# Filling the key stacks by way of HBM, and spreading a chunk's maxima evenly, in a two-layer perceiver kernel

## The reference

```python
x = x + _L0_xattn_ref(_layernorm(x), ctx_768, ...)   # q from x; k, v from the context; softmax over 12544
x = x + _L0_attn_ref(_layernorm(x), ...)             # Mamba
x = x + _L0_ffn_ref(_layernorm(x), ...)
x = x + _L1_xattn_ref(_layernorm(x), ctx_768, ...)   # the same shape of work again
x = x + _L1_attn_ref(_layernorm(x), ...)             # linear attention
x = x + _L1_ffn_ref(_layernorm(x), ...)
```

## Time and profile before

| | |
|---|---|
| median of three runs | 1404.1 us |
| the profiled execution's own time | 1412.64 us |
| its span | 1410.9 us |
| TensorE (PE) busy | 1151.9 us, 82% |
| VectorE (DVE) busy | 738.6 us, 52% |
| ScalarE (ACT) busy | 711.6 us, 50% |
| GpSimd (POOL) busy | 415.1 us, 29% |
| DMA moved | 147.04 MB, 104 GB/s over the span |

### The profile page before, as it was taken

One profiled execution on the slowest core, in us unless ns is written; L12 is line 12 of the kernel. 1 busy time (PEld: TensorE's weight loads), 2 busy tenths in 40 slices (PEclk: granted clock), 3 DMA queues, 4 the chain that ended last, 5 costly groups with the idle time before them and its releaser, 6 DMA issues.

```text
span 1410.9 us, 30285 instructions
## 1 busy us (share of the span) xinstructions
PE 1151.9 (82%) x13033; PEld 815.1 (58%) x13033; DVE 738.6 (52%) x1358; ACT 711.6 (50%) x991; POOL 415.1 (29%) x256
## 2 busy tenths in 40 slices
PE   6769899999999988315897769999999998989556
PEld 6446566666666645215696346666666666656345
DVE  4536565555565562678225536555555555563431
ACT  3336566666666546251212246666666666657210
POOL 3444444444444200042003444444443343300000
PEclk8689999999999999658898679999999999999668
DMA  7977777878787660610804977777777787760803
GB/s 147 140 104 98 99 101 104 108 100 111 104 111 98 72 148 2 210 60 3 295 1 96 135 109 97 100 104 103 101 105 101 99 110 100 86 120 2 297 24 64
DMA packets 88134, 147.04 MB, mean 104 GB/s; under 512 B 10040, under 2 KB 77568, under 8 KB 87488
## 3 DMA queue, kind: packets, MB, share of 16 engines
q1 hardware_dynamic: 87104, 144.98, 64.0%
q10 hardware_dynamic: 896, 0.12, 0.1%
HBM read 66.74 MB, written 0.18 MB: 47 GB/s over the span
## 4 chain that ended last, share of the span: by engine, by line
PE 65%; DVE 18%; issue 6%; DMA 5%; ACT 3%; POOL 2%; SPq 0%; ACTq 0%; DVEq 0%; POOLq 0%
PE ring L605 32%; PE st L605 16%; PE ot L605 15%; DVE mpart L1277 8%; DMA qst<-rowb 4%; DVE arena L1404 2%; PE ring L740 1%; ACT arena L983 1%; DMA arena<-scratch_perm 1%; DVE arena L1408 1%; DVE arena L1263 1%; DVE nmb L1285 1%; DMA wkv<-L_wkv 0%; SPq L398 0%; PE ring L611 0%
## 5 line engine op out<-in xcount | busy, mean ns | idle before, releaser
L1277 DVE TENSOR_REDUCE mpart<-ring 128x1 f32<-128x448 f32 x896 | 516.7, 619 | 435.2 <-PE ring L605 433.0
L1006 ACT ACTIVATE work<-st 128x1024 f32<-128x1024 f32 x392 | 401.6, 1024 | 242.9 <-PE st L605 236.7
L605 PE MATMUL ring<-arena,qst 96*128 96x448 bf16 x896 | 305.5, 375 | 12.5 <-issue 6.3
L605 PE MATMUL ot<-work,arena 128*17 128x128 f32 x6272 | 262.6, 284 | 29.2 <-issue 27.5
L605 PE MATMUL st<-qst,arena 97*128 97x128 bf16 x3136 | 249.6, 223 | 33.2 <-DMA qst<-rowb 18.1
L605 PEld LDWEIGHTS st<-qst,arena 97*128 97x128 bf16 x3136 | 202.2, 100 | 98.9 <-issue 42.7
L523 POOL TENSOR_TENSOR arena<-arena 128x896 f32<-128x896 f32 x52 | 98.2, 1888 | 519.4 <-ACT arena L979 519.4
L605 PEld LDWEIGHTS ot<-work,arena 128*17 128x17 f32 x6272 | 142.4, 99 | 131.6 <-issue 92.4
L605 PE MATMUL ring<-ctxr,wkvr 128*128 128x448 f32 x560 | 171.9, 451 | 38.5 <-POOL ctxr L554 24.2
L605 PE MATMUL ring<-wkvr,ctxr 128*128 128x256 f32 x980 | 150.4, 299 | 8.6 <-ACT arena L990 4.2
L605 PEld LDWEIGHTS ring<-ctxr,wkvr 128*128 128x128 f32 x560 | 124.8, 229 | 54.7 <-issue 34.2
(11 more groups left out here) (281 smaller groups left out, 787.2 us busy)
## 6 DMA issues: line engine op xcount, KB each, us to landing
arena<-arena SPq DMA_DIRECT2D x336, 224.0 KB, 11.2
arena<-ffn_W SPq DMA_DIRECT2D x16, 1024.0 KB, 12.1
warena<-ctxT SPq DMA_DIRECT2D x28, 448.0 KB, 14.2
warena<-ctxT SPq DMA_DIRECT2D x56, 224.0 KB, 14.9
arena<-f SPq DMA_DIRECT2D x2, 4096.0 KB, 25.0
arena<-scratch_bc SPq DMA_DIRECT2D x1, 2048.0 KB, 7.3
arena<-scratch_perm SPq DMA_DIRECT2D x2, 1024.0 KB, 9.7
arena<-rows SPq DMA_DIRECT2D x1, 1792.0 KB, 7.0
```

The costliest lines, as they stand in the source:

```text
L605: return nc.tensor.matmul(o, l, r, start=start, stop=stop, **kw)
L1006: nc.scalar.activation(pbuf[:, n % 2], st[:, 2 * (n % 2):2 * (n % 2) + 2].rearrange("p b k -> p (b k)"), ACT.Exp).then_inc(*signal(f"{lay} ...
L1277: V.reduce_max(mpart[:, 2 * h + hf:2 * h + hf + 1], ring[:, BANKS[step][0], 0:HALF], AX_X).then_inc(*signal(f"{lay}_b_max"))
```

## The change

The stack of a chunk is filled in two moves instead of one. First the three parts and two halves of `kparts` are written to a new tensor in HBM, `scratch_k` (two buffers), by six transfers of 128 rows of 1792 bytes. When all six have landed (`parts_out`), twelve transfers fill the stack from there, each one slot and one half of the heads: 16 rows of 14336 bytes, since in HBM the values of 8 heads lie one behind the other. The wait for the stack's old scores stands between the writes and the loads; before the writes stands a wait for the loads that last read this buffer of `scratch_k`. A half is now heads 0 to 7 or 8 to 15, so the maxima go in the plain order of heads and `head_of` is gone. ScalarE's `k1` waits for `parts_out` of the chunk before, once per chunk. And `per_unit` becomes (2, 3, 2, 3, 2, 2, 3, 2, 3) and (2, 2, 2, 2, 2): of a chunk's 32 maxima 10 instead of 17 are taken in units 9 to 13.

```diff
+PARTS = 16 * 3 * KC
...
-        per_unit = ((4,) * 8 + (0,) if c == 0 else (1, 1, 1, 1, 3, 2, 2, 2, 2)) + (3, 4, 3, 4, 3)
+        per_unit = ((4,) * 8 + (0,) if c == 0 else (2, 3, 2, 3, 2, 2, 3, 2, 3)) + (2, 2, 2, 2, 2)
...
-def head_of(n):
-
-    return n // 2 % (H // KC) * KC + n // H, n % 2
...
+        scratch_k = nc.dram_tensor("scratch_k", [2, 3, P, KC, CK], BF16).ap()
...
             def stack(lay, c):
 
                 b = c % KBUFS
+                if c >= 2:
+                    for half in range(2):
+                        sp.wait_ge(sem(f"{lay}_kst{half}_in"), STACK * (c - 1))
+                for part in range(3):
+                    for m in range(KC):
+                        sp.wait_ge(*of(lay, f"k{part + 1}_done", KC * c + m + 1))
+                        load(scratch_k[c % 2, part, :, m], kparts[:, part, m * CK:(m + 1) * CK], f"{lay}_parts_out")
                 if c >= KBUFS:
                     sp.wait_ge(sem(f"{lay}_s_full"), (c - KBUFS + 1) * UNITS)
-                for m in range(KC):
-                    for part in range(3):
-                        sp.wait_ge(*of(lay, f"k{part + 1}_done", KC * c + m + 1))
-                        for s in range(SLOTS):
-                            if K_SPLIT[s] == part:
-                                load(kst[HD * s:HD * (s + 1), b].rearrange("l (h m) k -> l h m k", m=KC)[:, :, m],
-                                     kparts[:, part, m * CK:(m + 1) * CK], f"{lay}_kst{m}_in")
+                sp.wait_ge(sem(f"{lay}_parts_out"), PARTS * (c + 1))
+                for half in range(2):
+                    heads = slice(half * H // 2, (half + 1) * H // 2)
+                    groups = slice(half * H // 2 // KC, (half + 1) * H // 2 // KC)
+                    for s in range(SLOTS):
+                        load(kst[HD * s:HD * (s + 1), b, heads].rearrange("l h k -> l (h k)"),
+                             scratch_k[c % 2, K_SPLIT[s]].rearrange("(l g) m k -> l g (m k)", l=HD)[:, groups]
+                             .rearrange("l g n -> l (g n)"), f"{lay}_kst{half}_in")
...
                     if kind == "b":
-                        h, hf = head_of(n)
+                        h, hf = n // 2, n % 2
...
                     if kind == "k1":
                         act.wait_ge(sem(f"{lay}_k_out"), 4 * c + 2 * n + 2)
-                        if c:
-                            act.wait_ge(sem(f"{lay}_kst{n}_in"), STACK * c)
+                        if n == 0 and c:
+                            act.wait_ge(sem(f"{lay}_parts_out"), PARTS * c)
...
-                        h, hf = head_of(n)
-                        V.reduce_max(mpart[:, 2 * h + hf:2 * h + hf + 1], ring[:, BANKS[step][0], 0:HALF], AX_X
+                        V.reduce_max(mpart[:, n:n + 1], ring[:, BANKS[step][0], 0:HALF], AX_X
```

## The result

The changed kernel took 1484.4 us (median of four runs, 1474.0 to 1493.8), the kernel before 1404.7 beside it. The ratio is 1.056, with a 95% interval of 1.047 to 1.065: slower by 5.6%, some 80 us. The forecast was 1493 us, 89 slower. The profiled execution has a span of 1479.6 us against 1410.9. The traces are of single executions; that of after_row_first (experiment 4) is 18 us slower than its median, and no wait is read from it.

A forecast was written before the change was run, and what follows sets the result against it. PE's work was taken to set most of the time, the rest short holes. Terms +29 +72 -19 -11 +18 = +89 took the profiled 1412.6 to 1501.7, which lies 8.5 above the median, giving 1493 us; range 1350 to 1590.

The forecast's parts named there:

- The rate of the loads: Stack loads from HBM: stay at 123 GB/s despite longer rows, because they write the same 16 partitions.
- Rival B: Stack loads: short rows were the cost, so loads run at 348 GB/s and the kernel takes 1307 us; chance 0.17.
- step 1: Writes of the key parts to HBM: six per chunk, 0.7 us each, 4 us of DMA time.
- Rival C: DMA queue: becomes the period if writes cost above 0.8 us each, giving 1595 us; chance 0.13.
- steps 2, 3: Stack loads per chunk: start 6.1 us later with both halves hidden; DMA time is 35 of 35.9 us.
- step 4: Next chunk's row of maxima: lands 1.2 us later behind context loads and first writes, +29 us in all.
- step 5: PE's instruction code fetches: wait longer behind the full DMA queue, +3 us a chunk, +72 us in all.
- Rival A: PE's instruction code: fetches wait as today, large rows change nothing for code, 1421 us; chance 0.28.
- step 6: Maxima spread evenly over the units: PE's weight loads are held less, -19 us in all.
- step 7: ScalarE before k1: no longer waits for stack loads, only for writes long done, -11 us.
- step 8: Start of each attention: all six writes must land before the stack's loads, +18 us for both attentions.

The follow-up runs named there:

- after_row_first: The changed kernel with the row step moved ahead of the second key cast of unit 10: 1441.3 us, ratio 1.028 to the kernel before.
- experiment 4: The row step moved ahead of the second key cast of unit 10, in the kernel before (1402.5 us) and in the changed kernel (1441.3 us).
- wide_loads: The changed kernel with the stack in final order in HBM, 12 writes and 2 loads into 96 partitions a chunk: 1377.1 us, ratio 0.984.
- maxima_row_first: The kernel before with the even spread and the row step ahead of the second key cast of unit 10: 1383.6 us, ratio 0.987.
- start_direct: The changed kernel with the first three stacks of each attention filled from SBUF as before: 1437.7 us, ratio 1.024 to the kernel before.
- route_alone: The changed kernel with the old spread of the maxima, so the route over HBM alone: 1442.6 us, ratio 1.031 to the kernel before.
- wide_old: wide_loads with the old spread of the maxima (the kernel before's per_unit): 1338.5 us, ratio 0.957 to the kernel before.

## Why the prediction was right, and which of its steps were not

The total came to +80 us for a forecast of +89. By the prediction's own steps:

- *The rate of the loads* was right, and it is the step that decided the case. The partitions written set the rate: 133 GB/s with long rows, about the same landing with short ones, 246 with 96 partitions. Rival B (short rows as the cost) is refuted.
- *Writes* (step 1) were right. By the DMA records they take 3.8 us of the 16 engines per chunk, 0.64 each, where 4 and 0.7 were predicted; SyncE issues them and the long-row loads in 0.3 to 0.46 us each (12 loads in 5.41 us), less than the 0.65 that I had for both, and the writes land in 2.2 us. Rival C, which needed more than 0.8 us each, falls with that.
- *Start of the loads and hidden halves* (steps 2, 3): the loads come 6.6 us after the row instead of with it, for 6.1 predicted. The queue does not become the period: with the route alone 22 steady chunks lose some 8 us in all.
- *The row* (step 4, +29): the route alone adds 21.7 us to these waits (39.8 against 18.1). The size was near, the reason only in part: the row lands 0.3 us later (median 2.0 against 1.7), not 1.2.
- *Fetches* (step 5, +72) is the term that was most mis-sized. PE's waits for issue grew by 24.8 us, with the route alone by 16.1 (67.2 in the three groups and 3.4 at another line, less 54.5). I expected over 100 us in all and found 79.3, of which late code is 64.7 against 53.6 before: +11. The holes are late code, as predicted. A full queue does hold the code back, as wide_loads shows, but the changed kernel's queue does so only a little more than the one before. Rival A, "fetches wait as today", was nearer for this term.
- *Maxima evenly* (step 6, -19) has the wrong sign in this kernel, and this is the step that failed. The gain that I worked out exists: 18 us, once the row is kept in front (maxima_row_first). What I left out is that the even spread lets TensorE finish the last scores of a chunk before ScalarE has copied the row, so that SyncE issues the stack first. Alone that costs 63 us. With the route over HBM the loads come later, so this race is not run, and yet the even spread costs 42 us there too (1484 against 1443). PE's waits for the row grew by 29.2 us with it (69.0 against 39.8) and those for issue by 8.7. The row's landing went from 2.0 to 2.4 us, and the cast of 0.94 us stands right before its copy; moving it gives 43 us back. That these two are all of it is argued and not shown.
- *k1's waits* (step 7, -11) for stack loads went: the list of ScalarE's waits after has none of them left. I did not test what that was worth.
- *The start* (step 8, +18) was too small: some 31 us by the row times, and 30 by start_direct.

The terms for the route, +29 +72 -11 +18, are +108, and the route alone cost 42. The term for the even spread is -19, and it cost some 40. An error of 66 us too much and one of some 60 too little made the total look good. That is luck. What was earned is "slower" for the route, which rests on the unchanged rate and the longer start.

What stays open: why the queue of long rows delays code more than the same bytes in short rows, and how the 42 us of the even spread on this route, and with them after_row_first's 43, divide.

## What to carry to other kernels

Before a transfer is reshaped, ask how many partitions it writes, not only how long its rows are: with the old spread of the maxima, a buffer in HBM already in the final order of all 96 partitions turned the same detour from a loss of 42 us into a gain of 62 (route_alone and wide_old). A small transfer that a whole stage waits for must be issued ahead of the bulk ones, and where only chance puts it there (0.3 us here) any change of balance can turn it round; look for such a race before evening out a schedule, and fix the order in the plan. When a forecast adds many terms, a right total proves none of them: run the two halves of a change apart.

## What the runs showed of the hardware that I had not expected

- A 4 KB transfer issued 0.67 us after the first of a run of 224 KB transfers into 16 partitions lands after 4.0 us; 0.3 us ahead of them it takes 1.7.
- SyncE issues a transfer of 16 rows from HBM or of 128 rows to HBM in 0.3 to 0.46 us, and one of 128 rows from SBUF to SBUF in 0.65.
- Code for TensorE arrives late here when the DMA engines are full for long: 53.6 us of holes that end 1.4 to 2.0 us behind a 16 KB code packet, with loads that fill the engines for some 23 us a chunk, and none of 1 us or more with loads that fill them for 12 (wide_loads).
